# Grouping the weights-times-values products of a causal attention stage on one Trainium2 core

## The reference, cut to what matters

```python
qkv = x @ Wqkv.T                                   # x normalised, (4, 1024, 128)
q, k, v = map(merge_heads, split(qkv, 3))          # each (4, 16, 1024, 8)
dots = einsum('bhid,bhjd->bhij', q, k) * 8 ** -0.5
dots = where(triu(ones, 1), -inf, dots)            # causal
attn = softmax(dots)
out = einsum('bhij,bhjd->bhid', attn, v)
x = x + merge(out) @ Wout.T + bout
```

## Time and profile before

| | |
|---|---|
| three runs | 1917.05, 1918.62 (median), 1921.89 us |
| profiled execution | span 1890.0 us from first to last instruction; the page has no other time of it |
| engines over the span | PE busy 86%, DVE 70%, ACT 49%, POOL 34% |
| 16 groups of the attention | from 342 to 884 us of the span |

### The profile page before, as it was taken

The page is one execution under the profiler, slowest core; times in us unless marked ns, Lnnn a source line. Parts: engine busy times, 40 slices in busy tenths (PEclk is TensorE's granted clock), DMA queues, the critical chain, the costliest instruction groups (busy, mean ns, idle before and its releaser), DMA issues. The chain is left out here.

```text
span 1890.0 us, 31524 instructions
## 1 busy us (share of the span) xinstructions
PE 1634.6 (86%) x10370; PEld 1161.7 (61%) x10375; DVE 1319.8 (70%) x2575; ACT 934.2 (49%) x1659; POOL 643.3 (34%) x802
## 2 busy tenths in 40 slices
PE   6999947999999999998799993675799999997576
PEld 5668835555555555554666783354578888886354
DVE  6635558888878788782754666898876666663897
ACT  2434423788888888885343442332244444443332
POOL 0787633111111111111088763232333333333232
PEclk9999978999999999999699997898799999999899
DMA  6123420111111111110513341001000000000000
GB/s 247 37 77 86 134 75 24 34 29 35 28 29 40 29 34 29 29 29 8 199 42 89 90 126 67 0 1 37 10 2 1 0 0 0 0 0 2 6 20 20
DMA packets 50298, 82.35 MB, mean 44 GB/s; under 512 B 11236, under 2 KB 35236, under 8 KB 49380
## 3 DMA queue, kind: packets, MB, share of 16 engines
q1 hardware_dynamic: 41092, 62.09, 11.5%
q0 software_dynamic: 9088, 18.76, 3.1%
HBM read 43.19 MB, written 31.22 MB: 39 GB/s over the span
## 5 line engine op out<-in xcount | busy, mean ns | idle before, releaser
L1928 DVE TENSOR_REDUCE z_parts<-z_pM 128x4 f32<-128x512 f32 x576 | 373.3, 685 | 98.3 <-PE z_pM L1666 94.6
L1843 ACT ACTIVATE z_Pr<-z_pE 128x512 f32<-128x512 f32 x576 | 322.4, 596 | 86.6 <-PE z_pE L1690 83.9
L1690 PE MATMUL z_pE<-z_QM,z_QK 128*128 128x512 f32 x576 | 250.8, 438 | 9.1 <-DMA z_QM<-z_Q 6.8
L2035 POOL TENSOR_SCALAR_AFFINE_SELECT z_Pr<-z_Pr 128x512 f32<-128x512 f32 x128 | 81.4, 636 | 483.8 <-ACT z_Pr L1843 483.8
L1666 PE MATMUL z_pM<-z_KM,z_Q 128*128 128x512 f32 x576 | 234.5, 411 | 1.5 <-DVE z_Q L1918 0.9
L1460 POOL TENSOR_TENSOR a_pm<-a_Pn,k_mask 128x512 f32<-128x512 f32 x128 | 132.2, 1058 | 233.5 <-PE a_pT L1299 153.4
L1690 PEld LDWEIGHTS z_pE<-z_QM,z_QK 128*128 128x128 f32 x576 | 108.0, 188 | 159.6 <-ACT z_Pr L1843 90.7
L493 POOL DMA_INDIRECT slot_results<-m_yq,m_xq x156 | 151.9, 974 | 73.8 <-ACT m_yq L698 41.7
L469 POOL DMA_INDIRECT slot_rows<-m_XN,m_dest x128 | 129.8, 1014 | 95.0 <-DVE m_dest L787 59.6
L1703 PE MATMUL z_pO<-z_Pr,z_V 128*9 128x512 f32 (+3 forms) x1536 | 159.3, 488 | 0.1
L1393 DVE TENSOR_SCALAR a_kz<-a_pk,s_bqk 64x512 f32<-64x512 f32 x128 | 95.9, 749 | 45.0 <-PE a_pk L1279 42.6
(11 more groups left out here) (294 smaller groups left out, 3770.6 us busy)
## 6 DMA issues: line engine op xcount, KB each, us to landing
slot_rows<-in_c_pad SPq DMA_DIRECT2D x2, 5070.0 KB, 23.5
m_xq<-slot_rows SPq DMA_DIRECT2D x38, 260.0 KB, 3.8
z_QM<-z_Q SPq DMA_DIRECT2D x128, 64.0 KB, 2.0
z_KM<-z_QK SPq DMA_DIRECT2D x60, 128.0 KB, 2.4
m_raw<-in_gu SPq DMA_DIRECT2D x2, 2048.0 KB, 8.6
m_XN<-slot_results SPq DMA_DIRECT2D x8, 512.0 KB, 4.3
m_raw<-slot_results SPq DMA_DIRECT2D x8, 512.0 KB, 5.4
slot_results<-m_yq,m_xq POOLq DMA_INDIRECT x156, 2.2
```

The source lines that it names most:

```text
L1690: mm(pE[e % 2][:, :].rearrange("p (h c) -> p h c", h=4), QK[G % RING][:, kt * P:(kt + 1) * P], QM[half][:, :, q * P:(q + 1) * P], start=Tr ...
L1843: a.activation(Pr[j % 4][:, :, q * P:(q + 1) * P], pE[e % 2][:, :].rearrange("p (h c) -> p h c", h=4), ACT.Exp, scale=DH0 ** -0.5).then_in ...
L1928: v.tensor_reduce(parts[:, qt, kb, :], pM[n % 3][:, :].rearrange("p (h k) -> p h k", h=4), AX.X, ALU.max).then_inc(maxed, 1)
L2035: g_.affine_select(blk, blk, [[0, 4], [1, P]], ALU.is_ge, 0.0, base=0, channel_multiplier=-1).then_inc(selected, 1)
```

## The change

One table differs. The 12 products of a group keep their order and their operands; they are issued in 8 places where there were 12. Products 1 and 2 move to step 13, 4 and 5 to step 20, 6 and 7 to step 28, 8 to step 33, 9 and 10 to step 37 (step 1 of the next group); 0, 3 and 11 stay.

```diff
-        AT_V = (8, 12, 13, 14, 19, 25, 31, 33, 35, 37, 39, 42)
+        AT_V = (8, 13, 13, 14, 20, 20, 28, 28, 33, 37, 37, 42)
```

## The result

The changed kernel takes 1940.13 us (median of 4 runs, 1936.66 to 1943.85) against 1918.46 us for the kernel before on the same chip (median of 4, 1917.05 to 1921.89): a ratio of 1.0114, interval 1.0095 to 1.0132. It is 21.7 us slower; 20.7 were forecast, 1939 us in all, in a range of 1928 to 1950.

The account below looks back on a forecast made before the run. PE bounds the kernel, with added E waits on ACT in bare steps outweighing saved switches. Terms 11 + 6 + 0.2 + 1.5 + 2 = +20.7 us take the span to 1910.7; plus 28.6 outside, 1939.3 us, range 1928 to 1950.

Parts of the forecast that it names:

- groups 4, 8, 12: Added wait of the first batch turn for DVE's output (0.71 us) and of M20 (0.2): +2.0 us each, +6.
- group 15: Last group: V's as cover in fewer places, only 2 switches saved: +2 us, bounds 1 to 3.
- rule of bare steps: Steps with something beside the E and M products cost no wait; two bare steps in a row cost 0.27 us.
- E13: PE's E product of step 13, after a bare pair: the plain wait of 0.27 us on ACT's exponential.
- E26: PE's E product of step 26, waiting for the exponential of step 24, delayed by keep_high: 0.39 us.
- E32: PE's E product of step 32; steps 29 to 33 repeat the pattern of steps 23 to 27: 0.42 us together.
- E35: PE's E product of step 35, opening the passage between groups, where 0.79 us of waits was forecast.
- E1: PE's E product of step 1, ending the passage between groups; waits 0.28 us for the exponential of step 35.
- Step 10: PE's wait for QM's DMA, chained from step 4, stays and hides nothing added before; 0.17 us more.
- the clock brings no term: In groups 14 and 15, despite their waits, the granted clock is 1.00 as in group 5: no effect.
- switches go and no wait comes: Rival: PE saves 19.2 us because ACT and DVE catch up behind the doubled V: 1899.4 us; chance 0.06.
- compounding backlog: Rival: DVE's longer bursts make M wait, then fills and E: another 1 to 2 us a group, 1955 to 1970; chance 0.06.

Follow-up runs that it names:

- merger at 12: Kernel before with products 1 and 2 both issued at step 12, the rest unchanged, 11 visits a group: 1885.1 us, ratio 0.9980.
- merger at step 8: Kernel before with product 1 joining product 0 at step 8, the rest unchanged, 11 visits a group: 1880.3 us, ratio 0.9945.
- earlier turn: Ten-visit kernel with the turn of the maximum moved from step 4 to 2, product 10 from 39 to 40: 1911.2 us, ratio 0.9914 to the kernel before.
- kernel with one V moved: Kernel before with product 5 moved from step 25 to step 22, nothing merged: 1894.5 against 1889.4 us, ratio 1.0032.
- pair-at-28 kernel: Kernel before with products 6 and 7 at step 28 instead of 31 and 33, the rest unchanged: 1905.4 against 1890.7 us, one run each.
- part-undone kernel: Changed kernel with product 8 put back from step 33 to step 35: 1921.3 us, one run.
- ten-visit kernel: Kernel before with products 0 and 1 at step 8, 2 and 3 at step 12, the rest unchanged: 1879.1 us, ratio 0.9953.

## Why the prediction was right, point by point

| term | forecast, us | measured in the traces, us |
|---|---|---|
| group with projections | +1.1 each, +11 in sum | +1.05 to +1.13 each, where no late DMA falls in; +11.4 in sum, with late ones on both sides |
| groups 4, 8, 12 | +2.0 each | +2.0, +2.0, +1.0 |
| group 0 | +0.2 | -0.5 |
| group 14 | +1.5 | +1.54 |
| group 15 | +2 (1 to 3) | +3.6 |
| attention | +20.7 | +21.0 |

The mechanism is the forecast one. That the sum came out within 0.3 us is in part luck: group 15 was 1.6 us too small, and group 0 (0.7) and group 12 (1.0) took it back for reasons that the prediction didn't have. Group 0 differs from trace to trace (35.49 us before, 34.35 with the merger at 12); why is open.

- **The rule of bare steps** held. By the starts in group 5 the added waits are 0.27 us at E4, 0.27 at E13, 0.38 at E26, 0.39 at E32, 0.84 from E35 to E1 and 0.16 at E10: 2.31 in sum, forecast 2.33. The period's +1.08 leaves 1.23 for the four switches, forecast 1.24. Seven experiments with other tables came out within 0.15 us of the group period that the theory had stated for them.
- **Groups 4, 8, 12**: the third is only +1.0 because its QM landed 1.0 us late in the trace of before and not after.
- **Step 10**: the wait stayed. From the start of M9 to that of E10's record it is 0.75 us in the changed kernel where it was 0.60; 0.17 more was forecast. That it is one chain from step 4 on is shown by the merger at step 8 and the earlier turn.
- **Group 15** is the term that was too small, and *the clock brings no term* is the sentence that failed. Stretches of the changed kernel's group 15 (the column behind POOL's is the granted clock):

```profile
886.70:900.00 13.30, 11.52 (x81) 4.99 (x81) 2.52 (x7) 9.53 (x18) 3.17 (x5) 1.00 0.09 21
900.00:902.90 2.90, 2.23 (x6) 0.80 (x5) 0.00 (x0) 2.71 (x7) 0.00 (x0) 1.00 0.00 0
902.95:906.30 3.35, 3.35 (x17) 0.56 (x17) 0.00 (x0) 1.12 (x2) 0.00 (x0) 0.50 0.00 0
906.40:908.00 1.60, 1.58 (x11) 0.88 (x7) 0.27 (x2) 0.67 (x2) 0.00 (x0) 1.00 0.00 0
```

PE had had little but E's and V's with pauses between them for 16 us, busy for 11.52 of the first 13.30 us and 2.23 of the next 2.90. Then the granted clock fell to the lower of its levels (1.2 GHz), and the doubled V of step 20 fell into this stretch. Below it, for comparison, the doubled V of step 28 in group 5:

```profile
903.50 3.30 PE L1703 MATMUL z_pO<-z_Pr,z_V 128*9 128x512 f32 x16
561.39 1.90 PE L1703 MATMUL z_pO<-z_Pr,z_V 128*9 128x512 f32 x16
```

3.30 us against 1.90 for 16 products of the same size: 1.4 of the missing 1.6 us. Whether the change brings the fall on isn't shown: group 15 has a mean clock of 0.95 in the kernel with one V moved too, and of 1.00 in the kernel before, in the pair-at-28 kernel and in the part-undone kernel.
- **The rivals.** That switches go and no wait comes is refuted by every table with bare pairs. Of the compounding backlog only the beginning shows. M's direct waits on DVE are 3.6 us in groups 1 to 14, 0.25 each. Once a group ACT's fill for M35 waits 0.54 us for DVE, in group 5 as in the others; before, such a wait came once in all:

```profile
567.86 0.60 ACT L1832 ACTIVATE z_pM<-k_after_query 128x512 f32<-128x512 bf16 x1 [0.54 <-DVE z_parts L1928]
ACT z_pM L1832 <- DVE z_parts L1928: 7.6, 14, 0.5
```

  The passage behind it took 0.84 us of wait where 0.79 was forecast, so hardly any of this reached PE. The Trainium skill says under TensorEngine Tiling (Array Packing), Key Properties, that a change of tiling mode drains TensorE. The merger at step 12 agrees in that one change less saves 0.32 us; by that rule alone the sign would have been wrong. The Trainium skill asks under Perfetto Trace Analysis, Optimizing Tensor Performance, that products rotate through PSUM banks so that the evacuation by ACT overlaps the next ones. With two tiles this overlap fails here for two bare steps in a row, by 0.27 us.
- **The start of the sum** was wrong though it did no harm: of the 28.6 us only some 1.8 lie around the span, the rest goes with the chip.

## What to carry to other kernels

In a queue that alternates short products into a ring of two with one consumer, work of another kind between them is not only overhead: it is the time in which the consumer answers. Count the steps with nothing in between before grouping such work, and group only where the step left bare stands alone. Put what is merged in front of a wait that runs anyway (here a DMA chain); as much of it as fits into the wait costs nothing (0.46 of 0.65 us here). All this was measured in one kernel.

## What the runs showed of the hardware

- **Instruction fetches and late DMAs go together.** QM's four transfers land after 2.0 us as a rule and after up to 3.7 in single groups. The late groups are those in which a block of instructions is fetched meanwhile. DMA traffic of the kernel before from the start of group 6 (late) and of group 5 (not late) up to step 10 (packets, MB, share of 16 engines):

```profile
q1 hardware_dynamic: 192, 0.26, 10.3%
q8 instruction: 1, 0.02, 0.7%
q14 instruction: 1, 0.01, 0.2%
...
q1 hardware_dynamic: 192, 0.26, 11.4%
```

  The same 192 packets stand in both, alone in the second. By the packets' own times, a block of 16 KB began 6.2 to 8.4 us after the group's start in groups 6, 9 and 12 of the kernel before, in 3, 6 and 9 of the changed one, and in 3, 6, 9 and 12 of the ten-visit kernel; QM's last packet ended 0.3 to 1.4 us late in exactly these and on time in all others. With the turn at step 2 the same transfer ran earlier, and the blocks at 7.9 and 8.2 us (groups 9 and 3) no longer met it: it was on time there, and late by 1.0 and 1.3 us in groups 6 and 12, whose blocks began at 4.2 and 6.2. Slow is the transfer that meets the block: in groups 3, 6 and 9 of the changed kernel the first two took 2.6 to 2.9 us, and SP issued the third 0.7 to 0.9 us late; in groups 6 and 12 of the kernel before the fourth took 3.7 and 3.0. Which engine's instructions are fetched, and how they hold up the others, was not tested.
- **Chips differ by more than the change.** The unchanged kernel took 1889.4 to 1926.0 us by chip. The attention starts 338.5 to 345.0 us into the traces from the chips with 1889.4 and 1890.7 us, and 359.1 us into the one from the chip with 1926.0. Outside the attention, the trace of the changed kernel is 27.5 us longer than that of before, most of it in the two mixtures of experts; the cause there stays open.
